# Loading the output projection's weights and inputs of a cross attention in seven pieces instead of in one burst

## The reference, cut to what matters

```python
q = _fq_sym(q, axis=-1); k = _fq_sym(k, axis=-1); v = _fq_sym(v, axis=2)
attn = jnp.einsum('bhqd,bhkd->bhqk', q, k)
attn = jax.nn.softmax(attn.astype(jnp.float32), axis=-1)
attn = _fq_unsigned(attn, axis=-1)
out = jnp.einsum('bhqk,bhkd->bhqd', attn, v)
out = jnp.transpose(out, (0, 2, 1, 3)).reshape(B, N, C)
return out @ Wp + bp
```

## Time and profile before

| | us |
|---|---|
| median of 3 runs | 3242.12 |
| lowest and highest | 3238.9, 3243.14 |
| the profiled execution's own time | 3242.31 |
| its span, first to last instruction | 3240.5 |
| `cross_heads`, from its first transposition to the last head's result | 632.9 to 1327.6 |

### The profile page before, as it was taken

How to read it: one execution, slowest core, us unless ns; L and a number is a source line. 1 busy time by engine, 2 the same in 40 slices (tenths; PEclk the granted TensorE clock), 3 DMA queues, 4 the chain that set the end, 5 groups by cost and what they waited for, 6 DMA issues and landing times. The chain is left out here.

```text
span 3240.5 us, 51881 instructions
## 1 busy us (share of the span) xinstructions
PE 2902.9 (90%) x19136; PEld 1909.6 (59%) x19136; DVE 2057.8 (64%) x2574; ACT 1528.2 (47%) x2911; POOL 992.6 (31%) x937
## 2 busy tenths in 40 slices
PE   7999699888888888779998999999975999989998
PEld 5666356444444444446665777777754566657776
DVE  4788656799999998651111299999997232324444
ACT  3444212499999988531111366666662111113343
POOL 0000044365666655420000176555575000000000
PEclk9999799899999999889999999999986999989999
DMA  2011222388888888620013111111112600200000
GB/s 88 27 33 33 99 72 78 76 166 168 168 168 169 170 163 179 167 98 26 26 40 106 40 46 53 53 53 53 46 46 106 113 29 30 66 20 14 26 26 27
DMA packets 497941, 256.57 MB, mean 79 GB/s; under 512 B 412112, under 2 KB 449616, under 8 KB 496208
## 3 DMA queue, kind: packets, MB, share of 16 engines
q1 hardware_dynamic: 487456, 247.66, 30.1%
q0 software_dynamic: 10288, 6.29, 1.3%
HBM read 121.65 MB, written 33.69 MB: 48 GB/s over the span
## 5 line engine op out<-in xcount | busy, mean ns | idle before, releaser
L1084 DVE TENSOR_REDUCE xh_top<-xh_seen 128x1 f32<-128x512 f32 (+1 forms) x768 | 631.9, 864 | 51.6 <-PE xh_seen L986 37.9
L1056 ACT ACTIVATE xh_prob<-xh_sc,xh_bias,xh_scale 128x1024 int16<-128x1024 f32 (+1 forms) x512 | 610.0, 1201 | 74.4 <-PE xh_sc L986 70.8
L1950 POOL TENSOR_TENSOR ss_state<-ss_du,ss_b_all 128x1024 f32<-128x1024 f32 x128 | 364.6, 2854 | 277.2 <-PE ss_turned L1670 200.3
L986 PE MATMUL xh_seen<-xh_kT,xh_qT 96*128 96x512 bf16 x1024 | 355.3, 389 | 80.2 <-DVE xh_top L1084 78.0
L1990 DVE TENSOR_TENSOR_SCAN ss_state<-ss_decay,ss_state 128x1024 f32<-128x1024 f32 x128 | 374.4, 2925 | 35.8 <-ACT ss_decay L1849 35.8
L986 PE MATMUL xh_sc<-xh_kT,xh_qT 96*128 96x512 bf16 x1024 | 310.5, 385 | 1.3 <-ACT xh_prob L1056 1.3
L1110 POOL CAST xh_probT<-xh_pairs 128x2048 int16<-128x2048 uint8 x128 | 241.8, 1889 | 17.5 <-DMA xh_pairs<-xh_prob 8.9
L1677 PE MATMUL ss_bank<-ss_xc,hold_w_conv 128*128 128x256 f32 x1024 | 235.2, 385 | 0.7 <-ACT ss_xc L1861 0.7
L986 PEld LDWEIGHTS xh_seen<-xh_kT,xh_qT 96*128 96x128 bf16 x1024 | 89.7, 97 | 240.9 <-DVE xh_top L1084 217.8
L1849 ACT ACTIVATE ss_decay<-ss_delta,ss_a 128x255 f32<-128x255 f32 x512 | 210.7, 496 | 25.6 <-DVE ss_state L1990 25.2
L1670 PE MATMUL ss_turned<-ss_ident,ss_state 128*128 128x128 f32 x1024 | 152.8, 296 | 65.8 <-DVE ss_acc L2001 64.1
(11 more groups left out here) (282 smaller groups left out, 4976.8 us busy)
## 6 DMA issues: line engine op xcount, KB each, us to landing
ss_b_all<-ss_states SPq DMA_DIRECT2D x8, 2048.0 KB, 7.0
xa_kT<-xp_kT SPq DMA_DIRECT2D x8, 768.0 KB, 5.9
xh_qT<-xa_qT SPq DMA_DIRECT2D x48, 128.0 KB, 3.3
xh_kT<-xa_kT SPq DMA_DIRECT2D x48, 128.0 KB, 3.4
sa_x<-in_x SPq DMA_DIRECT2D x8, 512.0 KB, 3.8
sa_y<-in_x SPq DMA_DIRECT2D x8, 512.0 KB, 4.5
x_after_self_attention<-sa_y_out SPq DMA_DIRECT2D x8, 512.0 KB, 3.0
xp_x<-x_after_self_attention SPq DMA_DIRECT2D x8, 512.0 KB, 6.4
```

Of the source, the lines that this page charges most:

```text
L986: ins = pe.matmul(out[:, c * D:(c + 1) * D], qT[s][:, t * P:(t + 1) * P], kT[s][:, at + c * D:at + (c + 1) * D], start=True, stop=True)
L1056: act.activation(out, scores, ACT.Exp, bias=bias[t % RING][:, :], scale=scale[s][:, t:t + 1], accum_out=total[s][:, half, t:t + 1]).then_i ...
L1084: ins = v.tensor_reduce(top[t % RING][:, k:k + 1], scores[:, 0:n], AX.X, ALU.max)\
L1950: g.tensor_tensor(state[k % RING][:, :, :], du[s][:, :, :], spread(b_all[s][:, k, :], KD), ALU.mult)\
```

## The change

The four DMAs behind tile 8 of head 14 are replaced by seven, one each behind the transpositions of tiles 0, 2, 4, 6, 8, 10 and 12 of the same head. The weights come in four DMAs of 256 KB (one for each group of 128 rows), then the bias (256 KB), then the two input tiles (512 KB each). The counts for which PE and POOL wait in the next stage grow accordingly, from 32 to 80. The total of 2304 KB and the queue stay the same. The piece of tile 4 is issued behind the six DMAs of the next head's `load`.

```diff
-                    if t == TT // 2 and h == H - 2:
-                        ahead.fetch(sp)
-                        ahead.fetch_inputs(sp)
+                    if h == H - 2 and t % 2 == 0 and t // 2 < ahead.pieces:
+                        ahead.fetch_piece(sp, t // 2)
...
-        def fetch(sp):
-            sp.dma_start(w[:, :, :], tiled(A["L0_xattn_Wp"])).then_inc(w_loaded, 16)
-            sp.dma_start(b[:, :], over_partitions(A["L0_xattn_bp"], D)).then_inc(w_loaded, 16)
-
-        def fetch_inputs(sp):
-            load_x(sp, 0)
-            load_x(sp, 1)
-
-        p.fetch, p.fetch_inputs, p.o, p.finish = fetch, fetch_inputs, heads_out, both_stored(stored, B // 2)
+        def fetch_piece(sp, i):
+
+            if i < KD:
+                sp.dma_start(w[:, i, :], tiled(A["L0_xattn_Wp"])[:, i, :]).then_inc(w_loaded, 16)
+            elif i == KD:
+                sp.dma_start(b[:, :], over_partitions(A["L0_xattn_bp"], D)).then_inc(w_loaded, 16)
+            else:
+                load_x(sp, i - KD - 1)
+
+        p.fetch_piece, p.pieces, p.o, p.finish = fetch_piece, KD + 3, heads_out, both_stored(stored, B // 2)
...
-            g.wait_ge(w_loaded, ONE + 32)
+            g.wait_ge(w_loaded, ONE + 16 * (KD + 1))
...
-            pe.wait_ge(w_loaded, ONE + 32)
+            pe.wait_ge(w_loaded, ONE + 16 * (KD + 1))
```

## The result

| | before | changed |
|---|---|---|
| median of 11 runs, us | 3239.82 | 3233.52 |
| lowest and highest, us | 3237.01, 3243.14 | 3230.8, 3236.53 |
| the profiled execution's own time, us | 3242.31 | 3233.05 |
| its span, us | 3240.5 | 3231.3 |

The ratio of the changed kernel to the one before is 0.9978, with a 95% interval of 0.9971 to 0.9986. The change makes the kernel faster by 0.22%, 6.3 us between the medians. Measured again beside other kernels, the ratio was 0.9982 (0.9973 to 0.9991).

A forecast was written before the change was run, and what follows sets the result against it. DVE was taken to set the pace at 42.53 us a head, DMA second, with a stall in head 14. 3242.31 - 6.39 + 0.3 = 3236.22 us, 3236.0 for the median; 8-in-10 range 3233.0 to 3240.5.

The forecast's parts named there:

- The sum: Whole kernel: 6.39 us removed and 0.3 us added, giving 3236.22 us profiled and 3236.0 us for the median.
- about 0.2%: Whole kernel: 6.5 us, so 3235.6 us, taken as what a measurement can tell from no change.
- within 0.2%: Whole kernel: chance 0.61, from the rest of the first case plus the second and third cases.
- faster: Whole kernel: gain beyond the 0.2% bound, chance 0.34, nearly half of the first case.
- The burst's removal, 6.39 us: Head 14, tile 9: the stall and the slow clock behind it go, gaining 6.39 us.
- 0.89 us per unit and 3.53 us of slack: SP's queue: 256 KB delays the next transposition by 0.89 us; an odd tile lands 3.53 us before POOL wants it.
- Tile 4, 0.3 us: Piece behind head 14's head load: tile 5 some 0.6 us late, costing 0.3 us, between 0 and 1.7.
- the rival of half a gain lost: Tile 5 comes 2.2 us late, 1.7 us lost, and a clock fall costs 2.34: 3239.8 us, chance 0.16.
- No backlog, 1.7 us idle per pair: Head 14's pieces: DMA idle 1.7 us per tile pair, so delays of 0.89 or 1.78 us carry over practically nothing.
- the forecast 2.8 to 3.9: Head 14: tile 9's transposition lands in about 2.8 to 3.9 us after its issue.
- Nothing for the three more issues: SP's queue: three more DMA issues of some 0.6 us each fit inside the slack, costing 0 us.
- Falls of the clock "will come in some executions": Either kernel: falls like head 13's, 2.34 us, come in some executions; 1.5 to 2 us put around the forecast.

The follow-up runs named there:

- e13: Kernel before, burst included, with DVE's softmax sums two tiles earlier (tile 3 in place of 5); median 3230.03 us, ratio 0.9966 to before.
- e2: Kernel before with its four DMAs whole but spread behind tiles 8, 10, 12 and 14 of head 14; ratio 0.9987 to before.
- e3: Changed kernel with six units of 256 KB (weights and one input) behind tile 8, bias behind 10, second input behind 12; one execution, 3239.35 us.
- e4: Changed kernel with all seven pieces behind the head load at tile 4 of head 14; one execution, 3243.96 us.
- e1: Changed kernel with its seven DMAs all behind tile 8 of head 14, split but not spread; ratio 1.0002 to before.
- e10: Changed kernel with DVE's addition and reciprocal of the softmax sums at tile 3 in place of tile 5 in every head; median 3224.4 us, ratio 0.9958 to before.
- e11: The changed kernel once more, unedited, measured beside e10 and the kernel before; median 3233.88 us, ratio 0.9982 to before.

## Why the prediction was right in its mechanism and wrong in its call

**The step that failed** is the one from the sum to the chances. The sum was 3242.12 - 6.39 + 0.3, a gain of 6.1 us. Measured are 6.3 us between the medians, and the ratio of 0.9978 (0.9971 to 0.9986) holds the forecast's 0.9981. But I set "about 0.2%" as what a measurement of this kernel can tell from no change and gave "within 0.2%" 0.61, for a gain that I had computed at 0.19%. No row stood behind that 0.2%. The measurement resolved 0.22% with about 0.08%, 2.4 us, on each side. A gain of 6 us isn't "the same" here, it is a small gain clear of noise, and "faster" should have had the largest chance, not 0.34.

**The basis** was high. The three runs that I had were 3238.9, 3242.12 and 3243.14 us; eleven runs have a median of 3239.82. The absolute 3236.0 was 2.5 us above the measured 3233.52, and 2.3 of them come from there. It lay in the range.

**The burst's removal, 6.39 us:** right. Head 14 takes 42.53 us. e13 shows that the size has 1.2 us of luck in it, by the time that the clock stays low.

**0.89 us per unit and 3.53 us of slack:** right for the burst. In e2 four units left nothing over, e3 and e4 give 0.78 us per unit beyond that. The reckoning left out the 0.23 us between a landing and POOL's start, small beside 3.53.

**Tile 4, 0.3 us:** measured 0 in one trace and 0.04 us in the other. The tile came just in time in the first and made POOL wait 0.58 us in the second, so the expected lateness of 0.6 us was near and its price was too high: head 14 swallowed it. The place was rightly named as the tight one, and the rival of half a gain lost was nearer than the result shows.

**No backlog, 1.7 us idle per pair:** wrong, though it cost nothing here. With 0.89 and 1.78 us of delay and nothing carried over, tiles 9, 11 and 13 should have had margins of 2.6, 1.75 and 1.75 us. They had 1.58, 0.93 and 0.74, and in the second trace tile 13 made POOL wait, where only tile 5 was named as able to. e2, which has the same bytes in half the tiles, shows what it costs when the backlog runs out of slack: about 2.2 us, the fall of the clock in that head left out. Here the 0.33 that the DMA share of 0.67 left couldn't all be filled. By the same token tile 9's transposition took 4.7 us to land, not the forecast 2.8 to 3.9.

**Nothing for the three more issues:** right. In e1 seven DMAs cost what four do. The Trainium skill (DMA: Bandwidth & Descriptors, "Anatomy of one DMA") has the fixed part of a DMA, on the GpSimd path, dominated by the latency of its completion; by that it wouldn't occupy the queue, and e1, on SP's queue, agrees.

**Falls of the clock "will come in some executions":** too weak, and the cause was not looked for. All eleven traces with the sums at tile 5 have one to five at heads' ends. They cost 1.3 to 2.3 us each; the first trace of the changed kernel loses 3.7 us by its two.

**What stays open.** The medians of e10 and e11 differ by 9.5 us, their two traces by 12.5: 6.56 in this stage, 3.2 behind it and 2.7 ahead of it, where the edit can't act. Why the stages behind it gain is open. That the pause has a part in the falls at the heads' ends is supported by no fall at 45 ends in three traces against 25 at 165 in eleven. It isn't the whole cause, since the same pause passes without a fall at the other 140; and the edit also moves DVE's two instructions and makes the head 0.25 us shorter, so that the wait of 0.53 us itself is what matters is argued, not shown. What picks the heads is open too.

## What to carry to other kernels

On a queue that also carries transfers someone waits for, count the bytes ahead of each of those against its slack (time wanted less time landed), and then count them again over several such transfers, because here the backlog was worked off more slowly than the mean DMA share suggested. Splitting a DMA did nothing here as long as the pieces stayed together; spreading did it, and the DMAs may stay whole where the queue gets time behind them. When a gain comes out near the noise, work out how many runs will be compared before calling it no change. And when the marks of a regular loop show single laps 1 to 2 us too long, look at what every lap does at that place: here moving two small VectorE instructions gained 9.5 us, more than the change, though 3 of them in a later stage and left unexplained.

## What the runs showed of the hardware that was not expected

The granted clock fell to 0.5, its 1.2 GHz level, behind pauses of PE as short as 0.53 us and 0.49 us, half a microsecond of work apart, at 25 of 165 heads' ends. It cost 1.3 to 2.3 us each time. With only the second pause left, no fall was seen at any of 45 heads' ends in three traces. The Trainium skill (TensorE: Matmul & The Clock Gate, "Loop structure matters more than you think") says that a copy out of PSUM by VectorE between groups of matmuls doesn't make PE go cold, as long as the next matmuls follow at once. Here they wait for that VectorE instruction, and the traces show falls at some of the heads.

The stall of 4.7 us was followed by a low clock of different length in two kernels, and cost 5.2 us in one and 6.4 in the other.
